# Another order of the experts' steps on TensorE, with longer durations in the planner, in an attention and mixture-of-experts kernel

## The reference

```python
x = x + attn(layernorm(x))        # theta, phi (64 wide), g: (theta phi^T) g / 16, no softmax
x = x + ffn(layernorm(x))         # the part below
# ffn: rmsnorm, q, k, v (16 heads, 4 kv heads of 16), rope, causal softmax, wo, residual,
#      rmsnorm, then 8 experts, 2 per token:
for e in range(8):
    g = silu(h @ w1[e].T) * (h @ w3[e].T)      # 256 -> 512
    out = out + (g @ w2[e].T) * wfull[:, e:e + 1]   # 512 -> 256
```

## Time and profile before

| | |
|---|---|
| median of 3 runs | 1093.17 us (1091.48 to 1096.17) |
| profiled execution, its own time | 1096.53 us |
| its span, first to last instruction | 1094.7 us |
| TensorE busy | 1042.8 us (95%) |
| VectorE, ScalarE, GpSimd busy | 754.0, 572.2, 424.2 us |
| mean granted TensorE clock | 0.991 of full speed |

### The profile page before, as it was taken

One profiled execution on the slowest core, in us unless ns is written; L12 is line 12 of the kernel. 1 busy time (PEld: TensorE's weight loads), 2 busy tenths in 40 slices (PEclk: granted clock), 3 DMA queues, 4 the chain that ended last, 5 costly groups with the idle time before them and its releaser, 6 DMA issues.

```text
span 1094.7 us, 18844 instructions
## 1 busy us (share of the span) xinstructions
PE 1042.8 (95%) x6124; PEld 627.3 (57%) x6124; DVE 754.0 (69%) x1753; ACT 572.2 (52%) x1180; POOL 424.2 (39%) x480
## 2 busy tenths in 40 slices
PE   7999999999999999999999999998989999999997
PEld 6765335564435333353333444465767888888886
DVE  4699999778788897798877798135686444444443
ACT  3564576547676987648766656671431222222221
POOL 1020232615632234421534323556655753333333
PEclk9999999999999999999999999998999999999999
DMA  6333113222325557623342521232333443222221
GB/s 190 123 99 118 49 49 113 86 87 85 85 90 165 180 172 207 191 76 108 103 121 71 136 55 44 60 89 59 83 85 65 100 87 58 47 47 49 49 44 11
DMA packets 85983, 102.24 MB, mean 93 GB/s; under 512 B 17120, under 2 KB 73568, under 8 KB 85888
## 3 DMA queue, kind: packets, MB, share of 16 engines
q1 hardware_dynamic: 71584, 81.39, 25.7%
q0 software_dynamic: 14304, 19.63, 9.4%
HBM read 56.15 MB, written 41.01 MB: 89 GB/s over the span
## 4 chain that ended last, share of the span: by engine, by line
PE 69%; DVE 18%; ACT 5%; issue 5%; POOL 1%; DMA 1%; SPq 0%; DVEq 0%; POOLq 0%; ACTq 0%
PE psum L2104 10%; PE psum L2048 10%; PE psum L2034 7%; DVE psum L1820 6%; PE psum L2090 5%; PE psum L2086 4%; PE psum L2088 4%; PE psum L2087 4%; PE psum L2014 3%; PE psum L2096 3%; PE psum L2000 3%; ACT probs_mem L1355 2%; DVE mx L1822 2%; PE psum L2055 2%; PE psum L2021 2%
## 5 line engine op out<-in xcount | busy, mean ns | idle before, releaser
L1355 ACT ACTIVATE probs_mem<-psum 128x512 f32<-128x512 f32 (+1 forms) x464 | 232.6, 588 | 92.8 <-PE psum L2034 92.4
L1820 DVE CUSTOM_DVE_ANT_1 psum<-psum,masking 128x640 f32<-128x640 f32 (+3 forms) x256 | 256.5, 1047 | 30.4 <-PE psum L2017 28.9
L1254 POOL DMA_INDIRECT out<-yout,labels x71 | 114.3, 1609 | 191.1 <-DVE yout L1912 98.3
L2034 PE MATMUL psum<-stack_mem 98*128 98x512 bf16 (+3 forms) x768 | 170.8, 327 | 7.6 <-DVE mx L1820 2.8
L1374 ACT ACTIVATE gated<-psum 128x512 f32<-128x512 f32 x71 | 42.4, 598 | 248.7 <-PE psum L2088 204.9
L1203 POOL TENSOR_SCALAR_AFFINE_SELECT probs_mem<-probs_mem 128x512 f32<-128x512 f32 x104 | 66.4, 639 | 237.0 <-ACT probs_mem L1355 236.7
L2104 PE MATMUL psum<-w_mem,gated 128*128 x568 | 134.7, 380 | 0.2
L2034 PEld LDWEIGHTS psum<-stack_mem 98*128 98x128 bf16 x768 | 64.7, 97 | 104.5 <-ACT probs_mem L1355 22.1
L2104 PEld LDWEIGHTS psum<-w_mem,gated 128*128 128x128 f32 x568 | 107.7, 190 | 23.3 <-issue 7.3
L1902 DVE SCALAR_TENSOR_TENSOR gated<-gated,psum 128x512 f32<-128x512 f32 x71 | 48.7, 686 | 103.9 <-ACT gated L1374 103.9
L2048 PE MATMUL psum<-probs_mem,v 128*17 128x512 f32 (+3 forms) x1152 | 116.0, 490 | 0.7 <-ACT heads_out L1362 0.2
(11 more groups left out here) (217 smaller groups left out, 1781.1 us busy)
## 6 DMA issues: line engine op xcount, KB each, us to landing
block<-routed SPq DMA_DIRECT2D x71, 129.0 KB, 2.1
w_mem<-in_w13T SPq DMA_DIRECT2D x16, 512.0 KB, 5.2
qk_parts<-w_mem SPq DMA_DIRECT2D x16, 384.0 KB, 2.6
stack_mem<-qk_parts SPq DMA_DIRECT2D x32, 192.0 KB, 3.3
w_mem<-in_x SPq DMA_DIRECT2D x8, 512.0 KB, 5.1
out<-w_mem SPq DMA_DIRECT2D x8, 512.0 KB, 4.1
x_late<-out SPq DMA_DIRECT2D x8, 512.0 KB, 5.0
stack_mem<-qk_parts SPq DMA_DIRECT2D x32, 128.0 KB, 2.7
```

Source lines behind the costliest of these rows:

```text
L1254: e.indirect_dma_start(out_rows, bass.IndirectOffsetOnAxis(ap=labels[w % NLABEL].bitcast(I32)[:, 0:1], axis=0), youts[w % NYOUT], None, bo ...
L1355: e.activation(probs[probs_of(m)][:, hh:hh + n, q0:CH], grid(turn[step][0][:, 0:n * (CH - q0)], n), ACT.Exp, scale=float(HD) ** -0.5).then ...
L1820: e.tensor_tensor_reduce(keys, keys, masked(w), 1.0, -3e38, ALU.add, ALU.max, to).then_inc(sem["max"], 1)
L2034: m = e.matmul(bk[:, i * (CH - q0):(i + 1) * (CH - q0)], s[0:STACK + NMAX, kt // TPR, GRP, kt % TPR * P:(kt % TPR + 1) * P], s[0:STACK + N ...
```

## The change

1. `experts()` lists a round as gatedT(w-1), up(w, 0), up(w, 1), blockT(w+1), down(w-1).
2. Durations in the plan: label 0.2 to 0.5, w13_hi 0.97 to 1.06, a split up product 0.66 to 0.69, w13_lo 2.8 to 4.4 on VectorE and 3.5 to 3.8 on GpSimd.
3. In the plan, gatedT(w) needs only TensorE's part of down(w-2), not its landing in DRAM. xnT(b) also needs q2_mm and v of batch b-2, and the loads of w13 and w2 also need v of the last batch (and x1_store).
4. Code for a split down product (`w2_hi`, `w2_lo`, `w2_part`, `g_hi`, `g_lo`) from block `DOWN_FROM` on. `DOWN_FROM = len(WORK) + 1` is 72, and blocks end at 70, so none of it is issued. Buffers for it are laid over others, and `wo_s` moves to another address.

```diff
+DOWN_FROM = len(WORK) + 1
...
-    "fetch": (("SP", 0.6),), "label": (("POOL", 0.2),), "gatedT": (("PE", 0.44), ("ACT", 0.49)), "w13_hi": (("ACT", 0.97),),
+    "fetch": (("SP", 0.6),), "label": (("POOL", 0.5),), "w13_hi": (("ACT", 1.06),), ...
...
-        took = sum(0.66 if is_split(w, half, k) else 0.87 for k in range(KD))
+        took = sum(0.69 if is_split(w, half, k) else 0.87 for k in range(KD))
...
-        return (("POOL", 3.5),) if at[1] else (("DVE", 2.8),)
+        return (("POOL", 3.8),) if at[1] else (("DVE", 4.4),)
...
-            return [("xn", b, 2 * at[1] + 1)]
+            return [("xn", b, 2 * at[1] + 1)] + [("q2_mm", b - 2, QR - 1), ("v", b - 2, 1)] * (b > 1)
...
-            return [("up", b, 1), pvs[ROOMY - 1]] + [("down", b - 2)] * (b > 1)
+            return [("up", b, 1), pvs[ROOMY - 1]] + [("first", "down", b - 2)] * (b > 1)
...
     def experts():
         n, steps = len(WORK), [("blockT", 0)]
         for w in range(n + 1):
-            steps += [("up", w, 0)] * (w < n) + [("gatedT", w - 1)] * (w > 0) + [("blockT", w + 1)] * (w + 1 < n)
-            steps += [("up", w, 1)] * (w < n) + [("down", w - 1)] * (w > 0)
+            steps += [("gatedT", w - 1)] * (w > 0) + [("up", w, 0)] * (w < n)
+            steps += [("up", w, 1)] * (w < n) + [("blockT", w + 1)] * (w + 1 < n) + [("down", w - 1)] * (w > 0)
...
         if i == 0:
+            done["first", *step] = end + DRAIN[engine]
```

More of the change, by code:

```diff
@@ L82 @@
 LO_PARTS = (slice(0, 5), slice(5, NE))
+DOWN_FROM = len(WORK) + 1
+W2_PARTS = (slice(0, 2), slice(2, KF))
 def is_split(w, half, k):
@@ L767, in mega_kernel @@
         x1 = [grid(x_even, TPB), grid(x_odd, TPB)]
+        x1_at = start_of()
         x1_late = sb("x1_late", [P, TPB * D]).rearrange("p (t c) -> p t c", t=TPB)
@@ L890, in mega_kernel @@
             "rank": lambda s: ("rank_out", 2 * nth[s]), "blockT": lambda s: ("blockT_out", nth[s]),
-            "up": lambda s: ("gated", nth[s]), "gatedT": lambda s: ("gatedT_out", nth[s]), "down": lambda s: ("y", nth[s])}
+            "up": lambda s: ("gated", nth[s]), "gatedT": lambda s: ("g_lo", nth[s] - DOWN_FROM) if s[1] >= DOWN_FROM else ("gatedT_out", nth[s]), "down": lambda s: ("y", nth[s])}
         turn, free = {}, {}
@@ L1246, in _ @@
                                     ALU.subtract).then_inc(sem["w13_lo_part"], 1)
+                elif stage == "w2_part":
+                    w, = at
+                    gi, c = WORK[w]
+                    part = slice(W2_PARTS[1].start * D, W2_PARTS[1].stop * D)
+                    q.wait_ge("route", routed(gi, "all"))
+                    q.wait_ge("w2_hi", w - DOWN_FROM + 1)
+                    if w > DOWN_FROM:
+                        q.wait_ge("down_mm", w)
+                    at_w = e.value_load(bexp[gi][0:1, c:c + 1], min_val=0, max_val=(NE - 1) * 2 * FFN)
+                    e.tensor_tensor(w2_lo[:, part], w2_mem[:, bass.ds(at_w + part.start, part.stop - part.start)], w2_hi[w % 2][:, part], ALU.subtract).then_inc(sem["w2_part"], 1)
                 elif stage == "down":
@@ L1890, in _ @@
                         e.tensor_tensor(x_lo[w % 2], got, x_hi[w % 2], ALU.subtract).then_inc(sem["blockT_out"], 1)
+                elif stage == "gatedT":
+                    w, = at
+                    q.wait_ge("g_hi", w - DOWN_FROM + 1)
+                    e.tensor_tensor(g_lo, turn[step][0], g_hi, ALU.subtract).then_inc(sem["g_lo"], 1)
+                elif stage == "w2_lo":
+                    w, = at
+                    gi, c = WORK[w]
+                    part = slice(W2_PARTS[0].start * D, W2_PARTS[0].stop * D)
+                    q.wait_ge("route", routed(gi, "all"))
+                    q.wait_ge("w2_hi", w - DOWN_FROM + 1)
+                    if w > DOWN_FROM:
+                        q.wait_ge("down_mm", w)
+                    at_w = e.value_load(bexp[gi][0:1, c:c + 1], min_val=0, max_val=(NE - 1) * 2 * FFN)
+                    e.tensor_tensor(w2_lo[:, part], w2_mem[:, bass.ds(at_w, part.stop)], w2_hi[w % 2][:, part], ALU.subtract).then_inc(sem["w2_lo"], 1)
                 elif stage == "w13_lo" and not at[1]:
```

73 lines of the change are left out of this document (61 added, 12 removed).

## The result

| | before | after |
|---|---|---|
| median of 20 runs, us | 1093.32 | 1095.74 |
| lowest run, us | 1088.92 | 1094.40 |
| profiled execution, own time, us | 1096.53 | 1095.69 |
| its span, us | 1094.7 | 1093.9 |
| its mean granted TensorE clock | 0.991 | 0.997 |

The ratio after to before is 1.0023, 95% interval 1.0012 to 1.0034: slower by 2.4 us, where 1.9 us less was forecast. Both are within the 0.5% that counted as no change. One execution of before took 1189.28 us and one beside the first experiments 2635.28; both are slow executions, and the ratios leave them out.

What follows compares the result with a forecast made beforehand. TensorE, busy 1042.8 of 1094.7 us, was taken to bound the kernel. Terms -4.7 + 2.4 + 0.8 - 0.4 = -1.9 us, from the median 1093.2, gave 1091.3 us, range 1085.5 to 1101.

Steps and rivals of the forecast that it cites:

- the four quarters: The four places where a quarter of the experts is converted: cost falls from 19.5 to 14.8 us, -4.7.
- What they cost now: At the four conversions after the change: 3.9, 3.6, 4.7 and 2.6 us of waits, load and warm steps, together 14.8.
- What they cost before: At the four conversions before the change: waits 10.1, warm steps 4.0, lower clock 5.4, together 19.5 us.
- The attention, +2.4: Last batch's attention: eleven new warm steps of 0.222 us each add 2.4 us, between 0 and +5.
- Rounds 13 to 20 with the raw copy, +0.8: VectorE's raw block copy ahead of x_lo uses up the load's margin: 0.13 us in each of six rounds, 0 to +2.
- The tail, 0: Rounds 22 to 70: a round stays 5.17 us with no idle time; no change, bounds 0 to +5 us.
- The end, -0.4: Ahead of the last gatedT: two warm steps of 0.222 us disappear, -0.4 us.
- The register load in every round: Slower rival: the load behind x_lo costs 0.2 us in each of 58 rounds, 1102.9 us; chance 0.17.
- The planned gaps are not real: Slower rival: 39 extra warm steps, 8.7 us, all stand in TensorE's way, 1098.5 us; chance 0.13.
- The quarters give more: Faster rival: waits at the conversions vanish, clock never falls, attention's warm steps fill real gaps, 1084.4 us; chance 0.13.

Runs made afterwards that it cites:

- the first experiments: The first four of twelve follow-up kernels, run on another chip with the kernel before beside them; its median there was 1093.38 us.
- before again: The kernel before, unchanged, run and profiled a second time: 1094.37 us, ratio 1.0011; this profile's span is 1090.9 us.
- durations_only: The changed kernel with the experts' order put back to that of before, 119 warm steps: 1092.69 us, ratio 0.9989.
- experiment 9: vector_only_new_order: the changed kernel with all eight experts of each quarter converted by VectorE, none by GpSimd: 1092.27 us, ratio 1.0002.
- experiment 6: The changed kernel without its 11 warm steps in the last batch's attention, the 50 at the quarters kept: 1099.0 us, ratio 1.0020.
- block_late_only: The changed kernel with gatedT(w-1) put back behind up(w, 0), blockT still behind both halves, 128 warm steps: 1114.78 us, ratio 1.0209.
- experiment 4: The changed kernel without the 61 warm steps between the first and last up product, 85 left: 1101.85 us, ratio 1.0080.
- gated_first_only: The changed kernel with blockT(w+1) put back behind up(w, 0), gatedT still first, 119 warm steps: 1094.36 us, ratio 1.0019.

## Why the prediction was wrong, step by step

**The step that failed** is the term of the four quarters, -4.7, which went wrong in both its halves.

*What they cost now* was forecast at 14.8 us and is 18.6. From block 7 to 24, which takes in the quarters and the rounds with the raw copy, -3.9 was forecast (-4.7 + 0.8). The change gives +0.1 against the profile that the prediction used and +2.0 against the other profile of before. The loss lies at the fourth quarter: blocks 20 to 24 take 26.21 us, against 24.22 and 23.96.

*What they cost before* was read from one execution, and the last step of the sum carried it over: "The profiled execution lies 3.4 above the median; the change is the same for both". Of the 19.5 us, 5.4 were lower clock by the prediction's own estimate, and the second profile takes 1.9 us less from block 12 to 24 with the same waits. A change that fills waits takes away just the part that made this execution slow, so that part cannot be subtracted from a median that mostly lacks it.

Profile against profile, -1.9 was forecast and the two spans give -0.8. That is luck: 1.6 of it lies before block 7, where the first profile of before had lost 2.0 us to the clock at 580 to 600 us, which the sum does not contain. Against the second profile of before the changed kernel is 3.0 us longer, and against the median 2.4. The range held the value, the sign did not.

| moment | before, profile shown | before again | after | durations_only |
|---|---|---|---|---|
| block 7 | 723.35 | 721.37 | 721.71 | 723.59 |
| block 12 | 758.00 | 756.01 | 756.67 | 758.24 |
| block 20 | 822.32 | 818.72 | 818.80 | 820.29 |
| block 24 | 846.54 | 842.68 | 845.01 | 843.19 |
| block 70 | 1083.93 | 1080.08 | 1083.09 | 1080.20 |

The last two columns differ by the order and the warm steps planned with it. From block 12 to 20 it costs 0.1 us, for the old order has the longer waits there (2.16, 0.78 and 3.91 us). From 20 to 24, the fourth quarter, it costs 3.3: the wait of 2.01, the lower clock behind it of 1.57 and two warm steps make 4.0, against a wait of 0.92. From 24 to 70 it costs 1.1. The 1.9 us by which the new order is ahead at block 7 are not explained; it is ahead there by 1.3 in experiment 9 too.

Then, term by term.

*The quarters, -4.7.* Forecast for now: 3.9, 3.6, 4.7, 2.6, together 14.8. Measured: first 0.70 + 0.24 + 3.11 = 4.05; second 0.57 ("issue") + 3.1 = 3.7; third 2.40 + 15 warm steps at 0.222 = 5.7; fourth 2.01 + 1.55 + 1.57 of lower clock = 5.1; together 18.6. The first two were right within 0.2. The other two missed the routing operation held up on VectorE and the scatters ahead of GpSimd's conversion, and with them the clock. The sum before also left out the wait of 1.07 us at 837.65, which is gone in after. And I did not see that at the second quarter the order takes cover away (experiment 9), and so why the plan had fourteen warm steps there.

*The attention, +2.4.* Too high: nothing can be measured in experiment 6, and the idle time is 2.8 us against 2.7. That fits the prediction's other reading, that VectorE sets the pace there. This error hid half of that in the quarters.

*Rounds 13 to 20 with the raw copy, +0.8.* Right in the sum, in three rounds and not six: 0.16 + 0.54 + 0.20 = 0.9.

*The tail, 0.* Nearly right: +0.7 us from block 24 to 70 against either profile of before (238.08 against 237.39 and 237.40), with no idle time. The round was judged at one place to 0.01 us; over 46 rounds it is 5.176 against 5.161. Why a round is 0.015 us longer the runs do not settle; both kernels with gatedT first, collision or not, have it (238.10 and 238.28).

*The end, -0.4.* Not seen: from block 70 to the end all three profiles take 10.8 us.

*The rivals.* The register load in every round did not come about; with x_lo's end at S + 1.32 a margin of 0.16 us was there (0.25 worked out), and block_late_only shows what happens when the product is wanted 0.43 us sooner. The Trainium skill's 64 entries for TensorE's queue (TensorE: Matmul & The Clock Gate, opening table) speak for a load that only the semaphore holds back. That agrees with 903.1 here, right behind x_lo, and the price appears in block_late_only all the same, since the product is wanted there before the load behind that semaphore can be done. "The planned gaps are not real" was wrong: experiment 4. "The quarters give more" did not come about.

In one line, from the medians' side: the new order costs 3 to 4 us more than the same durations with the old one, in these profiles at the fourth quarter and by the drift behind it, and the longer durations win back about 1 of it.

## What to carry to other kernels

Before a profile's idle time or low clock is entered as a gain against a median, ask whether that execution is a typical one: a clock lost in one profile is not there to be won in every run, and a second profile of the unchanged kernel tells. When a transpose or a load is moved later, look at every queue that it then stands behind at the rare long steps (here a conversion of 4.4 us), not only in the regular round. And where two engines take turns at one memory, try giving the work to one of them: here the split that looks like parallel work took 6.7 us where one engine takes 4.42.

## What the runs showed of the hardware

- VectorE and GpSimd take turns: VectorE converts 128x4096 in 4.42 us alone, while 128x2560 beside GpSimd's 128x1536 (4.01 us) takes 6.12 and 2.82 alone. The Trainium skill gives the reason (SBUF — State Buffer, section "SBUF: two separate sides": an exclusive lock held for the whole instruction); the traces agree.
- I had not expected how small an operation is held: 56 columns on VectorE took 3.84 us beside GpSimd's conversion, 0.22 when free, and 64 columns 3.38 in gated_first_only. It works the other way as well. In vector_only_new_order GpSimd's copy of 8 columns takes 3.66 us beside VectorE's conversion (750.67 to 755.09):

```profile
751.49 3.66 POOL L1231 COPY hrow<-ids_s 128x8 int32<-128x8 int32 x1
```

- From the end of x_lo to the first matmul behind a register load in block_late_only: 0.78 us (905.19 to 905.97), of which the load itself is 0.30 and the address arithmetic behind it 0.15.
- The same program with the same waits (11.2 and 11.1 us) was granted a clock of 0.991 in one profile and 0.994 in another, and took 3.8 us less. Over its executions the clock goes from 0.991 to 0.997, and the time from 1097.4 to 1089.1 us.
